# A macaron block on one core: the norm in two parts, the ranks behind an eviction, an earlier scatter signal, and earlier combines at the end

## The reference

```python
x = x + 0.5 * ffn(layernorm(x))
x = x + attn(layernorm(x))        # a selective state space scan, 16 states, 256 channels
x = x + 0.5 * ffn(layernorm(x))   # the same weights

def ffn(xt):                      # 8 experts, top 2, and 2 shared experts, hidden size 640
    scores = sigmoid(xt @ w_router.T)
    topk_w, topk_i = top_k(scores, 2);  topk_w = topk_w / sum(topk_w)
    expert(e) = (silu(xt @ wg[e].T) * (xt @ wu[e].T)) @ wd[e].T
    return sum over the two chosen of topk_w * expert + sum over the shared experts

def attn(x):                      # per batch, over time
    dt, B, C = softplus(xp[:256]), xp[256:272], xp[272:288]     # xp = x @ W_xproj.T
    h = exp(dt * A) * h + dt * B * x_t
    y = sum_n h * C + D * x_t
```

## Time and profile before

| | |
|---|---|
| Median of 3 runs | 547.87 us (546.45 to 549.91) |
| The profiled execution's own time | 546.11 us |
| Its span, first to last instruction | 544.2 us |
| TensorE matmuls | 522.5 us busy, 96% |
| TensorE weight loads | 422.4 us, 78% |
| VectorE / GpSimd / ScalarE | 327.8 us, 60% / 230.5, 42% / 156.9, 29% |
| DMA | 67.72 MB, mean 124 GB/s |

### The profile page before, as it was taken

One profiled execution on the slowest core, in us unless ns is written; L12 is line 12 of the kernel. 1 busy time (PEld: TensorE's weight loads), 2 busy tenths in 40 slices (PEclk: granted clock), 3 DMA queues, 4 the chain that ended last, 5 costly groups with the idle time before them and its releaser, 6 DMA issues.

```text
span 544.2 us, 11101 instructions
## 1 busy us (share of the span) xinstructions
PE 522.5 (96%) x4386; PEld 422.4 (78%) x4387; DVE 327.8 (60%) x654; ACT 156.9 (29%) x336; POOL 230.5 (42%) x208
## 2 busy tenths in 40 slices
PE   8999999999979999999979999999997999999996
PEld 7998997458958888447979788964487999954695
DVE  3843526422555999997686399999768232522224
ACT  1111122221117445443202643554421011222210
POOL 1041100322303999995453189999700540000031
PEclk9999999999999999999989999999999999999999
DMA  7986993912204445540321436556100230210012
GB/s 225 398 322 227 394 381 133 316 60 59 70 11 130 114 136 144 152 118 25 105 68 69 118 101 121 133 145 154 34 21 2 98 88 29 78 40 13 20 55 74
DMA packets 41991, 67.72 MB, mean 124 GB/s; under 512 B 5041, under 2 KB 24753, under 8 KB 41937
## 3 DMA queue, kind: packets, MB, share of 16 engines
q1 hardware_dynamic: 29968, 40.75, 25.7%
q10 hardware_dynamic: 8400, 16.12, 8.0%
q0 software_dynamic: 3568, 10.10, 5.5%
HBM read 48.74 MB, written 18.22 MB: 123 GB/s over the span
## 4 chain that ended last, share of the span: by engine, by line
PE 53%; DVE 15%; POOL 14%; issue 10%; DMA 4%; ACT 2%; POOLq 0%; SPq 0%; DVEq 0%; ACTq 0%
PE ps L513 18%; PE ps L528 10%; PE ps L538 10%; POOL region L954 7%; PE ps L551 6%; POOL xnt L968 5%; DVE ps L1035 3%; DMA xg_rows<-region,pos 2%; PE ps L661 2%; PE ps L562 2%; DVE hb L990 2%; PE ps L713 1%; PE ps L683 1%; DMA region<-yg_rows,ypos 1%; PE ps L557 1%
## 5 line engine op out<-in xcount | busy, mean ns | idle before, releaser
L513 PEld LDWEIGHTS ps<-xt,w_gu 128*128 128x128 f32 x1360 | 156.3, 192 | 13.7 <-ACT xt L770 5.6
L513 PE MATMUL ps<-xt,w_gu 128*128 128x128 f32 x1360 | 161.3, 277 | 4.5 <-DVE xres L1005 2.8
L990 DVE SCALAR_TENSOR_TENSOR hb<-hb,ps 128x640 f32<-128x640 f32 x68 | 55.5, 816 | 134.3 <-ACT hb L752 134.0
L538 PE MATMUL ps<-w_dn,hb 128*128 128x256 f32 x520 | 122.1, 383 | 0.0
L538 PEld LDWEIGHTS ps<-w_dn,hb 128*128 128x128 f32 x520 | 96.0, 193 | 11.2
L752 ACT ACTIVATE hb<-ps 128x640 f32<-128x640 f32 x68 | 47.4, 698 | 173.6 <-PE ps L513 167.2
L513 PE MATMUL ps<-xnt,w_gu 128*128 128x128 f32 x720 | 86.3, 279 | 5.5 <-DVE xres L1005 5.5
L513 PEld LDWEIGHTS ps<-xnt,w_gu 128*128 128x128 f32 x720 | 84.8, 195 | 7.5 <-DVE xres L1005 5.9
L968 POOL TENSOR_TENSOR xnt<-xnt,hh 128x512 f32<-128x512 f32 x64 | 81.8, 1278 | 1.3 <-DVE hh L1040 1.3
L935 POOL DMA_INDIRECT region<-yg_rows,ypos x32 | 30.6, 955 | 116.4 <-DMA yg_rows<-ob 94.8
L1035 DVE TENSOR_TENSOR_SCAN ps<-ps,region 128x512 f32<-128x512 f32 x64 | 78.2, 1223 | 0.9 <-POOL region L954 0.7
(11 more groups left out here) (104 smaller groups left out, 329.7 us busy)
## 6 DMA issues: line engine op xcount, KB each, us to landing
bcb<-bc_rows SPq DMA_DIRECT2D x22, 512.0 KB, 5.0
region<-bc_rows SPq DMA_DIRECT2D x10, 512.0 KB, 5.3
xg<-xg_rows SPq DMA_DIRECT2D x34, 128.0 KB, 3.6
w_gu<-in_wg ACTq DMA_DIRECT2D x6, 640.0 KB, 7.1
w_gu<-in_wu ACTq DMA_DIRECT2D x6, 640.0 KB, 8.5
w_dn<-in_wd ACTq DMA_DIRECT2D x6, 640.0 KB, 9.2
yg_rows<-ob SPq DMA_DIRECT2D x20, 128.0 KB, 4.1
xg_rows<-bcb SPq DMA_DIRECT2D x1, 2176.0 KB, 15.2
```

Source lines behind the costliest of these rows:

```text
L513: last = nc.tensor.matmul(gup(p)[:, c * P:(c + 1) * P], w_gu4[:, e, k, c * P:(c + 1) * P], x, start=(k == 0), stop=(k == KC - 1))
L538: ins = nc.tensor.matmul(outp(p), hb[:, p, c * P:(c + 1) * P], w_dn4[:, e, c, :], start=(c == 0), stop=(c == IC - 1))
L990: nc.vector.scalar_tensor_tensor(out=h, in0=h, scalar=1.0, in1=gup(p)[:, 0:I], op0=ALU.add, op1=ALU.mult).then_inc(s_a, 1)
```

## The change

1. **The norm in two steps.** `N` becomes `N1` (statistics, `ve`, the power on GpSimd) and `N2` (Newton step, the writes, the store of the rows). The P norms keep both together. In the A norms a tile's eviction, and for half 1 also hidden(35), stands between them. For half 0, hidden(18) now comes ahead of the combine of token tile 3.
2. **The ranks behind the eviction.** `R2` of segments 2 and 3 comes after `second` of tile 32 and 49. The combines of segment 1 are one block behind tile 33.
3. **`route_rows`.** The two choices' last operations are interleaved with fewer links, and a new semaphore `s_dest` is raised when `pos` is written, ahead of `ypos` and the table; the scatter waits for it instead of `s_pos`.
4. **The end.** Two combines of segment 3 stand ahead of hidden(67), two ahead of the eviction of tile 66.
5. **The scan.** VectorE's first state stands ahead of the first scan tile's work; ScalarE's order is as before.

```diff
-    ("tiles", S1 - 2, S1 - 1), ("C", 0, 0, 2), ("tiles", S1 - 1, S1), ("C", 0, 2, TT), ("N", "A", 0),
-    ("tiles", S1, S1 + 1), ("first", S1 + 1), ("T", "A", 0), ("second", S1 + 1), ("X1", 0),
+    ("tiles", S1 - 2, S1 - 1), ("C", 0, 0, 2), ("tiles", S1 - 1, S1), ("C", 0, 2, 3), ("first", S1), ("C", 0, 3, TT),
+    ("N1", "A", 0), ("second", S1), ("N2", "A", 0), ("first", S1 + 1), ("T", "A", 0), ("second", S1 + 1), ("X1", 0),
...
-    ("first", S1 + 15), ("R2", 2), ("S", 2, 0), ("second", S1 + 15), ("C", 1, 0, 2),
-    ("tiles", S2 - 1, S2), ("C", 1, 2, TT), ("N", "A", 1), ("S", 2, 1),
-    ("tiles", S2, S2 + 1), ("first", S2 + 1), ("T", "A", 1), ("second", S2 + 1), ("X1", 1),
+    ("tiles", S1 + 15, S1 + 16), ("R2", 2), ("S", 2, 0), ("tiles", S2 - 1, S2), ("C", 1, 0, TT), ("N1", "A", 1),
+    ("S", 2, 1), ("tiles", S2, S2 + 1), ("N2", "A", 1), ("first", S2 + 1), ("T", "A", 1), ("second", S2 + 1), ("X1", 1),
...
-    ("first", S2 + 15), ("R2", 3), ("S", 3, 0), ("S", 3, 1), ("G", 2), ("second", S2 + 15),
+    ("tiles", S2 + 15, S2 + 16), ("R2", 3), ("S", 3, 0), ("S", 3, 1), ("G", 2),
...
-    ("tiles", S3 + 13, TILES - 2), ("first", TILES - 2), ("C", 3, 0, 3), ("second", TILES - 2), ("C", 3, 3, TT),
+    ("tiles", S3 + 13, TILES - 2), ("C", 3, 0, 2), ("first", TILES - 2), ("C", 3, 2, TT), ("second", TILES - 2),
...
-                    pool.wait_ge(s_pos, s + 1)
+                    pool.wait_ge(s_dest, s + 1)
...
-                for j, one in enumerate((one1, one2)):
-                    link(nc.vector.tensor_tensor(one[:, :, :], one[:, :, :], eq[:, :, :], ALU.mult))
-                    link(nc.vector.tensor_reduce(kk[:, :], one[:, :, :], AX.X, ALU.add))
-                    link(nc.vector.tensor_scalar(pos[:, s, j, :], kk[:, :], float(TT * P), None, ALU.add))
-                    link(nc.vector.tensor_copy(ypos[:, s, j, :], kk[:, :]))
-
+                nc.vector.tensor_tensor(one1[:, :, :], one1[:, :, :], eq[:, :, :], ALU.mult)
+                link(nc.vector.tensor_tensor(one2[:, :, :], one2[:, :, :], eq[:, :, :], ALU.mult))
+                nc.vector.tensor_reduce(m1[:, :], one1[:, :, :], AX.X, ALU.add)
+                link(nc.vector.tensor_reduce(m2[:, :], one2[:, :, :], AX.X, ALU.add))
+                nc.vector.tensor_scalar(pos[:, s, 0, :], m1[:, :], float(TT * P), None, ALU.add)
+                nc.vector.tensor_scalar(pos[:, s, 1, :], m2[:, :], float(TT * P), None, ALU.add).then_inc(s_dest, 1)
+                nc.vector.tensor_copy(ypos[:, s, 0, :], m1[:, :])
+                nc.vector.tensor_copy(ypos[:, s, 1, :], m2[:, :])
...
                     for n in range(start, last):
-                        states(start, n, 0, h)
+                        ahead, behind = half_states(start, n, 0), half_states(start, n, 1)
+                        if n == start:
+                            ahead, behind = behind[:1], behind[1:]
+                        states(ahead, h)
                         body(n)
-                        states(start, n, 1, h)
+                        states(behind, h)
```

More of the change, by code:

```diff
@@ L132 @@
 SCHEDULE = [
-    ("N", "P", 0), ("T", "P", 0), ("R1", 0), ("start",), ("R2", 0), ("S", 0, 0), ("S", 0, 1),
-    ("tiles", 0, 6), ("N", "P", 1), ("tiles", 6, 8), ("T", "P", 1), ("tiles", 8, 9), ("R1", 1),
+    ("N1", "P", 0), ("N2", "P", 0), ("T", "P", 0), ("R1", 0), ("start",), ("R2", 0), ("S", 0, 0), ("S", 0, 1),
+    ("tiles", 0, 6), ("N1", "P", 1), ("N2", "P", 1), ("tiles", 6, 8), ("T", "P", 1), ("tiles", 8, 9), ("R1", 1),
     ("tiles", 9, 10), ("R2", 1), ("S", 1, 0), ("S", 1, 1), ("tiles", 10, S1 - 2), ("O", 0), ("G", 0),
-    ("tiles", S1 - 2, S1 - 1), ("C", 0, 0, 2), ("tiles", S1 - 1, S1), ("C", 0, 2, TT), ("N", "A", 0),
@@ L137 @@
-    ("tiles", S1, S1 + 1), ("first", S1 + 1), ("T", "A", 0), ("second", S1 + 1), ("X1", 0),
-    ("scan", S1 + 2, S1 + 13, 0), ("first", S1 + 13), ("Y", 0), ("N", "P", 2), ("second", S1 + 13),
+    ("tiles", S1 - 2, S1 - 1), ("C", 0, 0, 2), ("tiles", S1 - 1, S1), ("C", 0, 2, 3), ("first", S1), ("C", 0, 3, TT),
+    ("N1", "A", 0), ("second", S1), ("N2", "A", 0), ("first", S1 + 1), ("T", "A", 0), ("second", S1 + 1), ("X1", 0),
+    ("scan", S1 + 2, S1 + 13, 0), ("first", S1 + 13), ("Y", 0), ("N1", "P", 2), ("N2", "P", 2), ("second", S1 + 13),
@@ L139 @@
     ("O", 1), ("G", 1), ("first", S1 + 14), ("T", "P", 2), ("second", S1 + 14), ("R1", 2),
-    ("first", S1 + 15), ("R2", 2), ("S", 2, 0), ("second", S1 + 15), ("C", 1, 0, 2),
-    ("tiles", S2 - 1, S2), ("C", 1, 2, TT), ("N", "A", 1), ("S", 2, 1),
-    ("tiles", S2, S2 + 1), ("first", S2 + 1), ("T", "A", 1), ("second", S2 + 1), ("X1", 1),
-    ("scan", S2 + 2, S2 + 13, 1), ("first", S2 + 13), ("Y", 1), ("N", "P", 3), ("second", S2 + 13),
+    ("tiles", S1 + 15, S1 + 16), ("R2", 2), ("S", 2, 0), ("tiles", S2 - 1, S2), ("C", 1, 0, TT), ("N1", "A", 1),
@@ L144 @@
+    ("S", 2, 1), ("tiles", S2, S2 + 1), ("N2", "A", 1), ("first", S2 + 1), ("T", "A", 1), ("second", S2 + 1), ("X1", 1),
+    ("scan", S2 + 2, S2 + 13, 1), ("first", S2 + 13), ("Y", 1), ("N1", "P", 3), ("N2", "P", 3), ("second", S2 + 13),
     ("first", S2 + 14), ("T", "P", 3), ("second", S2 + 14), ("O", 2), ("R1", 3),
-    ("first", S2 + 15), ("R2", 3), ("S", 3, 0), ("S", 3, 1), ("G", 2), ("second", S2 + 15),
+    ("tiles", S2 + 15, S2 + 16), ("R2", 3), ("S", 3, 0), ("S", 3, 1), ("G", 2),
     ("tiles", S2 + 16, S3 + 6), ("C", 2, 0, TT), ("tiles", S3 + 6, S3 + 13), ("O", 3), ("G", 3),
-    ("tiles", S3 + 13, TILES - 2), ("first", TILES - 2), ("C", 3, 0, 3), ("second", TILES - 2), ("C", 3, 3, TT),
+    ("tiles", S3 + 13, TILES - 2), ("C", 3, 0, 2), ("first", TILES - 2), ("C", 3, 2, TT), ("second", TILES - 2),
@@ L160, in last_ahead_of_overflow @@
             return last
-NORM = {key: k for k, key in enumerate(x[1:] for x in SCHEDULE if x[0] == "N")}
+NORM = {key: k for k, key in enumerate(x[1:] for x in SCHEDULE if x[0] == "N1")}
 def build(nc, x_in, alog_in, d_in, wx_in, wr_in, wg_in, wu_in, wd_in, sg_in, su_in, sd_in,
@@ L309, in build @@
         s_pos = sem("s_pos")
+        s_dest = sem("s_dest")
         s_sc = [sem(f"s_sc{s}") for s in range(SEGS)]
@@ L1028, in overflow, with states @@
                     dve.sem_inc(s_none, 1)
-            def states(first, n, part, h):
-                for g in half_states(first, n, part):
+            def states(those, h):
+                for g in those:
                     m, d = g // KC, g % KC
@@ L1041, in states, with variance @@
                                             ALU.mult).then_inc(s_hc, 1)
-            def norm(k, kind, half):
+            def variance(k, kind, half):
                 src = xres[:, half * TT:(half + 1) * TT, :]
@@ L1053, in norm @@
                 nc.vector.tensor_scalar(ve[:, :], mv[:, :, 1], 1e-5, None, ALU.add).then_inc(s_var, 1)
+            def norm(k, kind, half):
+                src = xres[:, half * TT:(half + 1) * TT, :]
                 dve.wait_ge(s_pow, k + 1)
@@ L1166, in _ @@
                 kind = step[0]
-                if kind == "N":
-                    half = step[2] % 2
+                if kind == "N1":
                     if step[1:] == ("P", 1):
@@ L1172, in _ @@
                         dve.wait_ge(s_ev, (step[2] + 1) * SEG_TILES)
-                    norm(NORM[step[1:]], step[1], half)
+                    variance(NORM[step[1:]], step[1], step[2] % 2)
+                elif kind == "N2":
+                    norm(NORM[step[1:]], step[1], step[2] % 2)
                 elif kind == "R1":
```

3 lines of the change are left out of this document (2 added, 1 removed).

## The result

The changed kernel takes **530.85 us** (median of 4 runs, 530.5 to 530.96) against 548.02 (4 runs, 546.45 to 549.91) for the kernel before beside it: ratio 0.970, 95% interval 0.9668 to 0.9732. The forecast was 533.2. Its profiled execution took 530.95 us with a span of 528.9, against 546.11 and 544.2. By the profiles the change brings 15.2, where the sum had 13.6.

What follows compares the result with a forecast made beforehand. TensorE, busy 96%, was taken as the bound, waiting for VectorE's evictions behind tiny operations. 3.1 + 4.1 + 4.6 + 1.8 + 0 = 13.6 off 546.11 gave 532.5, plus 0.7: 533.2; range 530.0 to 538.5.

Steps and rivals of the forecast that it cites:

- rival 3: Something beside the ranks holds the evictions: the stalls stay and only the gain at the end comes, 544.3; chance 0.04.
- b: Ranks of segment 2, then the norm of half 1: 4.1 us gained, 4.6 less 0.5 waiting; ends 3.4 and 4.6.
- c: Ranks of segment 3: gate and up of tile 52 starts 4.6 us sooner, half-clock stretch included.
- a: Scan norm of half 0, around tile 17: TensorE's wait goes, 3.1 us gained; 2.6 if the norm still holds transposes.
- The rule against it: Chained VectorE operations can't be sped up by leaving out semaphores; by it b would be 3.5, the sum 0.6 smaller.
- the full 1.7: Clock's share of the gain at b and c, 1.7 us each, taken whole; its other end was nothing.
- The end: VectorE's last combines and evictions: two combines move into idle time, last write out 1.8 us sooner; other end 1.3.
- Rival 2: The moved state costs the scans: hidden(20) is late, each of 22 tiles loses 0.2, +4.4, 537; chance 0.08.
- rival 4: In the scans the early state shifts VectorE against GpSimd, one wait per tile: 28 us lost, 560.6; chance 0.03.
- Rival 1: New waits replace the old at b and a: loss 2 to 5 us, 534.5 to 537.5; chance 0.2.
- Costed at nothing: Split P norms and shorter ranks of segments 0 and 1: no gain; ranks worth 0.65 each without the clearing DMA's cover.
- The 0.7 added for the runs: Added to the forecast since the runs' median, 547.87, was 1.8 above the profile: some may be stalls the change removes.

Runs made afterwards that it cites:

- after_again: The changed kernel run again unaltered, as yardstick for the first set of variants: 533.32 us (6 runs), ratio 0.9725 to the kernel before.
- after_c3: The changed kernel run once more unaltered, as control for the last set of variants: 535.05 us (6 runs), ratio 0.9736 to the kernel before.
- all_linked: The changed kernel with a wait after each of the eight operations before the table in `route_rows`: 531.31 us (5 runs), ratio 0.9724 to the kernel before.
- ranks_ahead: The changed kernel with the ranks of segments 2 and 3 ahead of the eviction again: 538.29 us (6 runs), 7.4 over the control.
- kept_busy: The kernel before with six extra matmuls, results unused, in each of TensorE's two waits behind the ranks: 546.58 us (12 runs), ratio 0.9956 to the kernel before.

## Why the prediction was right, and where it was not

**The mechanism, and rival 3.** The mechanism is shown: the evictions were held by the ranks and the norm. Putting only these back brings the waits back at b and c (2.0 each) and at a (1.46). Rival 3 (only the end is gained) falls with that.

**a: 3.1, measured 3.11.** The changed kernel's time axis is 1.3 ahead here (149.15 and 147.85 for the same product). On it the eviction was forecast to end at 150.95 - 1.3 = 149.65 and ended at 149.64; the norm's second part at 151.7 - 1.3 = 150.4, and it began at 150.48. The transposes had no wait in this trace. In `after_again` and `after_c3` they had (0.19 and 0.71), and there a brings 2.75 and 2.23: the 2.6 that the prediction had as the other end. So that the best case came was luck of the execution.

**b: 4.1, measured 4.55.** The failed part is the 0.5 of waiting for the norm. VectorE's block ended sooner than worked out. The forecast counted on before's time axis, which is 4.4 ahead here (274.0 and 269.58 for the same product): eviction of tile 34 at 290.9 - 4.4 = 286.5, measured 285.94; norm at 293.0 - 4.4 = 288.6, measured 288.06. The ranks' saving was sized 0.65 and measured 0.78 (1.71 to 0.93); most of the rest is the block of combines with the norm's first part, 6.6 in the forecast (282.3 to 288.9) and 6.3 in the trace. `all_linked` shows how near it was: with 0.8 more on VectorE the transposes end 0.7 later. Within the range that the prediction gave for b, 3.4 to 4.6, the mis-sized term is this 0.5, which measured 0.

**The rule against it.** The operations of 128x32 that follow with no wait between them start 0.11 apart, with one 0.22, and those of 128x4 0.07 against 0.20 (`pos` and `ypos`, 274.61 to 274.68). The measurement decides against what the Trainium skill (VectorE: DVE Perf Modes, "The DRAIN you can't avoid") says of operations chained without semaphores; by it the two kernels would show the same 1.71.

**c: 4.6, measured 4.55.** In this trace the clock never fell. `ranks_ahead` splits it and b: 4.0 for two waits, and 3.4 that goes with a lower clock, as much as two falls of 1.7. The positions stood 1.16 ahead of the table and not the 1.9 of the prediction; nothing hung on it here.

**The clock's price is a matter of the execution.** I took the full 1.7 twice because before's profile had it twice. That is right for that profile, and for most runs of before: (1 - 0.992) x 548 = 4.4 for the median of the controls, more than the 3.4 of two falls. The other half of the reasoning, "after the 2.84 of a it did not fall", described one execution: in `kept_busy` it fell there.

**The end: 1.8, measured 2.02.** Against the order of before put back, the traces beside it show 1.7. With an end of 7.95 to 8.24, as in five of the ten traces, it brings 1.3 to 1.6: near the prediction's other end, 1.3.

**The scans: 0, measured -0.22.** Rival 2 (4.4 lost) and rival 4 (28 lost) are refuted: with the state behind, the stages are the same to 0.5. Rival 1 (new waits over 1 us) didn't come in full: in the first trace the largest new wait is 0.32, once in each scan, and in the others 0.71, at a, where the rival had 0.5 to 1.

**The failed step**, besides the 0.5 at b, is the line "Costed at nothing: ... the first scatter waits for the clearing DMA, not for positions". The row of GpSimd's first scatter names `table` as what ended its idle time (28.18, 16.69 of waiting), and TensorE waited 0.87 for tile 6 at 51.17. I had read TensorE's waits by their totals, where 0.87 for a DMA is a small line, and did not follow it back. It is the larger part of the head's 1.3. Not all of it is the early signal: the prediction allowed a gain of 0.65 from the shorter ranks "if that cover were gone", and they gave 0.79 of room here, the signal 1.16; and `kept_busy`, with neither, had no wait at all. That the scatter waited for the ranks is shown, how much of the wait a typical execution saves is open. Another 0.3 is the start of TensorE's work (10.66 instead of 10.96 for the first transposes), which moves between executions of the changed kernel (9.89 to 11.21) and is luck; the last 0.1 was not followed.

**The 0.7 added for the runs** did not come in this comparison: the median, 530.85, is at the profiled execution's 530.95. That is no rule for the changed kernel. Its controls spread over 3.0 to 4.8 and had medians of 533.32, 530.93 and 535.05, so how near 533.2 comes to a median is in part a matter of chip and execution. The gain in medians that the forecast implied, 547.87 - 533.2 = 14.7, lies among the controls' 14.2 to 15.8. For the first comparison: 1.3 head, 0.45 b, 0.2 end, -0.2 scans are the 1.7 that the sum missed, 0.7 the rest.

## What to carry to other kernels

An in-order engine that owes another one a buffer should pay it before a long chain of small operations, and inside that chain wherever it waits for a third engine. Follow every DMA wait of the bound engine, small ones too, back to the signal that issued its first link: a signal raised for the last output of a block delays those who need only the first. In a kernel like this one, price a wait of 2 to 2.8 us on TensorE at its own length, plus up to 1.7 of clock that comes and goes between executions. One trace of a change shows one draw of the waits that hang on transfers: here a, the end and the head each came out at their best in the first.
